# A four-layer graph network on one core: loading x ahead of more of the adjacency, transposing it later, and starting the second layer's rows before the first layer's last row tiles are evicted

## The reference

```
h = relu(layernorm(x))                      # layer 0
A = (adj != 0)
x = x + (A @ (h @ W + b)) / A.sum(axis=0)[:, None]
h = relu(layernorm(x))                      # layer 1
adj_hat = adj + I
d = adj_hat.sum(axis=1) ** -0.5
x = x + relu((adj_hat * d[:, None] * d[None, :]) @ (h @ weight))
```

## Time and profile before

| what | value |
|---|---|
| device time, median of 3 runs | 1339.97 us (1336.94 to 1341.37) |
| span of the profiled execution (first to last instruction) | 1337.7 us |
| PE busy | 1271.0 us, 95% |
| DVE busy | 1010.9 us, 76% |
| ACT busy | 629.3 us, 47% |
| POOL busy | 365.4 us, 27% |
| mean granted TensorE clock | 0.990 |

### The profile page before, as it was taken

The page is one execution under the profiler, slowest core; times in us unless marked ns, Lnnn a source line. Parts: engine busy times, 40 slices in busy tenths (PEclk is TensorE's granted clock), DMA queues, the critical chain, the costliest instruction groups (busy, mean ns, idle before and its releaser), DMA issues.

```text
span 1337.7 us, 26725 instructions
## 1 busy us (share of the span) xinstructions
PE 1271.0 (95%) x9548; PEld 947.8 (71%) x9548; DVE 1010.9 (76%) x2273; ACT 629.3 (47%) x1480; POOL 365.4 (27%) x422
## 2 busy tenths in 40 slices
PE   4899999998999999989999999999999987899998
PEld 3688888873455555557776777776767665688887
DVE  6899999939455555579988978978889987776642
ACT  3486644715322222266556755756666653311111
POOL 1100000013322222223323323332323222465433
PEclk8899999999999999999999999999999999999999
DMA  9999999702112210125653553543545414350500
GB/s 235 255 333 330 401 402 394 305 25 78 36 61 64 63 56 25 48 71 166 195 172 119 170 174 111 176 149 135 182 118 167 135 57 111 87 150 25 150 25 25
DMA packets 122898, 199.93 MB, mean 149 GB/s; under 512 B 13200, under 2 KB 83856, under 8 KB 122768
## 3 DMA queue, kind: packets, MB, share of 16 engines
q1 hardware_dynamic: 115568, 194.04, 45.6%
q10 hardware_dynamic: 7200, 4.20, 1.1%
HBM read 147.85 MB, written 50.33 MB: 148 GB/s over the span
## 4 chain that ended last, share of the span: by engine, by line
PE 69%; issue 13%; DVE 7%; POOL 6%; DMA 2%; ACT 1%; SPq 1%; ACTq 0%; POOLq 0%; DVEq 0%
PE ps L1817 10%; PE ps L1613 8%; PE ps L1614 8%; PE ps L1575 8%; PE ps L1576 8%; PE ps L1726 7%; PE ps L1711 5%; PE ps L1712 5%; POOL ring L687 4%; PE ps L1778 3%; PE ps L1743 2%; DMA acc<-in_adj 2%; DVE ring L789 1%; PE ps L1592 1%; POOL small L680 1%
## 5 line engine op out<-in xcount | busy, mean ns | idle before, releaser
L687 POOL TENSOR_TENSOR ring<-ring 128x512 f16<-128x512 f32 (+3 forms) x133 | 152.1, 1150 | 326.5 <-ACT ring L1487 326.5
L1575 PE MATMUL ps<-val_hi,ring 128*128 128x257 f16 x1024 | 227.1, 274 | 0.0
L1576 PE MATMUL ps<-val_lo,ring 128*128 128x256 f16 x1024 | 226.8, 273 | 0.0
L1613 PE MATMUL ps<-ring,acc 128*128 128x512 fp8e4 x512 | 194.1, 379 | 5.4 <-DVE acc L926 5.3
L1726 PE MATMUL ps<-hnt 128*128 128x512 f16 (+3 forms) x864 | 196.5, 364 | 1.0 <-DVE ring L1035 1.0
L1614 PE MATMUL ps<-ring,acc 128*128 128x512 fp8e4 x512 | 194.0, 379 | 0.0
L789 DVE STREAM_TRANSPOSE ring<-acc 128x1024 uint8<-128x1024 uint8 x128 | 151.4, 1219 | 20.4 <-DMA acc<-in_adj 20.2
L1711 PE MATMUL ps<-val_hi,ring 128*128 128x257 f16 x490 | 136.1, 278 | 18.9 <-POOL ring L687 12.9
L1711 PE MATMUL ps<-val_hi,hs 128*128 128x257 f16 x534 | 145.8, 273 | 0.9 <-DVE acc L1098 0.6
L1743 PE MATMUL ps<-val_hi,hs 128*128 128x257 f16 x534 | 145.8, 273 | 0.0
L1712 PE MATMUL ps<-val_lo,hs 128*128 128x256 f16 x534 | 145.6, 273 | 0.0
(11 more groups left out here) (234 smaller groups left out, 2377.3 us busy)
## 6 DMA issues: line engine op xcount, KB each, us to landing
acc<-in_adj SPq DMA_DIRECT2D x256, 256.0 KB, 7.5
turned_dram<-ring SPq DMA_DIRECT2D x56, 512.0 KB, 2.9
ring<-turned_dram SPq DMA_DIRECT2D x224, 128.0 KB, 2.9
at_dram<-ring SPq DMA_DIRECT2D x32, 512.0 KB, 8.9
ring<-at_dram SPq DMA_DIRECT2D x64, 256.0 KB, 4.0
ring<-at_dram SPq DMA_DIRECT2D x24, 512.0 KB, 3.9
ring<-at_dram SPq DMA_DIRECT2D x9, 1024.0 KB, 9.6
xs<-in_x SPq DMA_DIRECT2D x12, 256.0 KB, 12.3
```

The costliest lines, as they stand in the source:

```text
L687: nc.gpsimd.tensor_tensor(lo2[m % 2][:, k:GW], p2t[m % 2][:, k:GW], hi2[m % 2][:, k:GW], ALU.subtract).then_inc(sem["lo2_done"], 1)
L1575: nc.tensor.matmul(ps[:, k % 8, 0:D + 1], lhs, val_hi0[:, t, 0:D + 1], start=(t == 0), stop=False)
L1576: last = nc.tensor.matmul(ps[:, k % 8, 0:D], lhs, val_lo0[:, t, :], start=False, stop=(t == NB - 1))
L1613: nc.tensor.matmul(ps[:, bank + c, :], g_hi[:, t, c * P:(c + 1) * P], src, start=(t == 0), stop=False)
```

## The change

Both ends of layer 0 are edited.

First stage: SP's queue becomes x0, weights, x1, half 0, **x2**, half 1, **x3**, half 2, half 3, half 4 and so on. The quarters stand at the steps of a table `QUARTER_STEPS`: 9, 11, 15, 16, then one a step from 18 to 33, and two each in 34 and 35 (24 quarters, tiles 0 to 5). Tiles 6 and 7 and the two DVE column sums of group 0 follow the loop. An early tile is opened two steps after its last quarter (steps 18, 23, 27, 31 in place of 9, 13, 17, 21). ACT's 24 column sums of group 0 all stand behind the loop; before, they began at step 21.

Between the layers: DVE evicts only tiles 26 and 27 ahead of the degrees and the rows; tiles 28, 29, 30 and 31 are evicted after `low1` of batches 1, 3, 4 and 5. Before, 26 to 30 stood ahead of the rows, and 31 after batch 1. On POOL, `inverse_root` of the last group moves from before batch 3 to before batch 8, and the two `add_identity` from before batch 5 to behind the last batch.

```diff
--- before.py
+++ after.py
@@ -205,9 +205,16 @@
         ASUMS = NB - 4 * DSUMS
 
 
-        def quarters_by(s):
-
-            return s // 2 if s < 8 else s - 4
+        QUARTER_STEPS = (9, 11, 15, 16) + tuple(range(18, STEPS0)) + (STEPS0 - 2, STEPS0 - 1)
+        EARLY_TILES = len(QUARTER_STEPS) // 4
+
+        def quarters_in(s):
+
+            return [n for n, step in enumerate(sorted(QUARTER_STEPS)) if step == s]
+
+        def tile_step(b):
+
+            return sorted(QUARTER_STEPS)[4 * b + 3]
 
         def early_blocks():
 
@@ -216,7 +223,7 @@
             while total < GB * NB:
                 s, mine = len(table), []
                 for _ in range(5 if s < STEPS0 else GB * NB):
-                    open_b = [b for b in range(GB) if s >= 4 * b + 9 and progress[b] < min(NB, s - 4)]
+                    open_b = [b for b in range(GB) if s >= tile_step(b) + 2 and progress[b] < min(NB, s - 4)]
                     if open_b:
                         b = min(open_b, key=lambda b: (progress[b], b))
                         mine.append((b, progress[b]))
@@ -453,11 +460,11 @@
                 sp.dma_start(xs[32 * a:32 * a + 32, GB:8, :], x_q[a, :, GB:8, :]).then_inc(x_loaded[0], 16)
             load_x(sp, 1, (0, 2, 1, 3))
             load_half(sp, 0, (0, 2, 1, 3))
+            load_x(sp, 2, (0, 2, 1, 3))
             load_half(sp, 1, (0, 2, 1, 3))
-            load_x(sp, 2, (0, 2, 1, 3))
+            load_x(sp, 3, (0, 2, 1, 3))
             load_half(sp, 2, (0, 2, 1, 3))
             load_half(sp, 3, (0, 2, 1, 3))
-            load_x(sp, 3, (0, 2, 1, 3))
             for h in range(4, NH):
                 sp.wait_ge(sem["tr_done"], 2 * (h - 4) + 2)
                 load_half(sp, h, (0, 2, 1, 3))
@@ -638,14 +645,13 @@
                     inverse_root(g)
             inverse_root(NG - 2)
             for i, (t, n) in enumerate(batches1):
-                if i == 3:
+                if i == 8:
                     inverse_root(NG - 1)
-                if i == 5:
-                    add_identity(0)
-                    add_identity(1)
                 pool.wait_ge(sem["var1_ready"], i + 1)
                 nc.gpsimd.tensor_tensor(rstd4[i % 2][:, 0:n], ve4[i % 2][:, 0:n], half[:, 0:n],
                                         ALU.pow).then_inc(sem["rstd1_ready"], 1)
+            add_identity(0)
+            add_identity(1)
             pool.wait_ge(sem["r3_clamped"], 1)
             nc.gpsimd.tensor_tensor(f3, f3, half, ALU.pow).then_inc(sem["r3_ready"], 1)
 
@@ -816,15 +822,16 @@
             for s in range(STEPS0):
                 if s + AHEAD0 < NB:
                     stats0(s + AHEAD0)
-                for n in range(quarters_by(s), quarters_by(s + 1)):
+                for n in quarters_in(s):
                     transposed(n // 4, n % 4)
                 if s % GB == 2 and s // GB + 1 < NG:
                     shift0(s // GB + 1)
                 if 3 <= s < NB + 3:
                     low0(s - 3)
-                if s in (24, 30):
-                    column_sums(0, (s - 24) // 6, GW)
-
+            for k in range(EARLY_TILES, 8):
+                for i in range(4):
+                    transposed(k, i)
+                column_sums(0, k - EARLY_TILES, GW)
 
             dve.wait_ge(sem["w12_loaded"], 32)
             for l in (1, 2):
@@ -870,7 +877,7 @@
                     column_sums(k // GB - 1, k % GB, GW)
             dve.wait_ge(sem["tr_done"], 4 * NB)
             nc.vector.tensor_reduce(last_sum, at_bits[3][:, :, 3 * P:GW], AX.X, ALU.add).then_inc(sem["deg_step"], 1)
-            for k in range(NB - 6, NB - 1):
+            for k in range(NB - 6, NB - 4):
                 saved0(k)
 
 
@@ -925,14 +932,15 @@
                     dve.wait_ge(sem["hi1_ready"], t + 1)
                     nc.vector.tensor_tensor(g_lo[:, t, :], h1[t % 4], g_hi[:, t, :], ALU.subtract).then_inc(sem["g_ready"], 1)
 
+            saved_after = {1: NB - 4, 3: NB - 3, 4: NB - 2, 5: NB - 1}
             stats1(0)
             scales1(0)
             for i in range(len(batches1)):
                 if i + 1 < len(batches1):
                     stats1(i + 1)
                 low1(i)
-                if i == 1:
-                    saved0(NB - 1)
+                if i in saved_after:
+                    saved0(saved_after[i])
                 if i + 1 < len(batches1):
                     scales1(i + 1)
 
@@ -1383,9 +1391,7 @@
                         act.wait_ge(sem["wsc_ready"], 1)
                     nc.scalar.activation(val_hi0[:, t, 0:D], ps[:, 6 + t % 2, 0:D], ACT.Copy,
                                          scale=wsc).then_inc(sem["hi0_done"], 1)
-                if s >= 21:
-                    column_sum(0, 8 + s - 21, GW)
-            for t in range(24, NB):
+            for t in range(4 * DSUMS, NB):
                 column_sum(0, t, GW)
 
             for h in range(16, NH):
```

## The result

The changed kernel took 1318.19, 1320.16, 1320.20, 1339.48 and 1347.34 us: a median of 1320.20 against 1339.97 (both are medians of five executions, not of three as the section on the metric has it). The comparison leaves out executions more than 1.5% above the fastest, so its ratio of 0.984 (95% interval 0.982 to 0.987, about 1318.8 us) rests on the three lower ones. The same kernel timed a second time (run e1) took 1320.43 to 1342.21 us, six executions with a median of 1332.91 against 1341.2, ratio 0.991 (0.987 to 0.994). Over both times the eleven executions have a median of 1328.2, and five of them lie above 1337. The kernel before stayed between 1332 and 1351 beside every run, but for two outliers (1495.98 and 5717.65), with medians of 1338.8 to 1341.2. So the change is a gain of some 20 us in some executions and of nothing in others. Why it is both is the question of this study.

What follows compares the result with a forecast made beforehand. PE, busy 95% of the span, was taken as the bound. Gains of 10.4 us in layer 0's first stage and 5.3 between the layers, 15.7 in all, took 1339.97 to 1324.3 us; range 1319 to 1333.

Steps and rivals of the forecast that it cites:

- M(2): PE's projection early in layer 0's steps: forecast to start at 16.0 us in place of 22.68.
- The four half-clock steps: Layer 0's steps on PE: four assumed at half clock, 2.27 us each in place of 1.25, putting projection 17 at 43.5.
- lower bound of 41.4: Earliest start forecast for projection 17 on PE, 41.4 us, with only two half-clock steps right after the restart.
- the clock stays full: Rival for layer 0's steps: full clock after the restart, projection 17 at 41.4, total 1322.2 us; chance 0.17.
- M(17) to M(31), and the postponed pairs: Later steps of layer 0: 30.5 us between these projections; 36 more pairs follow afterwards, giving back 7.9 us.
- The cover: Layer 0 after the steps: DVE has adjacency tiles ready at least 10 us before PE wants them.
- The lead of the rows: Between the layers: DVE releases row tile 4 at 287.2, PE wants it at 292.5, a 5.3 us lead.
- DVE is late for the rows: Rival between the layers: lateness of DVE's last quarter beyond the 5.3 us lead is lost; chance 0.1.
- D of 10: Example lateness in us of DVE's last quarter of layer 0, giving a total of 1329.0 to 1330.3.
- The second part: Between the layers: later evictions and identity remove PE's waits for `low1`, a gain of 5.3 us.
- The slower rival: Layer 0's load stream: its low rate lasts longer, last quarter over 21 us late, the change loses; chance 0.04.

Runs made afterwards that it cites:

- e8: Changed kernel plus eight unread 512 KB DRAM-to-DRAM copies on SP's queue, one behind each of halves 24 to 31: median 1339.18 us.
- e4: Changed kernel with the old load order, x2 back behind half 1 and x3 behind half 3: median 1332.40 us.
- e11: Changed kernel with the later layers' weights loaded early and the cast adjacency's stores spread behind every second half: median 1324.49 us.
- e10: Changed kernel with each group's four stores of cast adjacency spread behind every second half: median 1330.41 us.
- e13: Changed kernel with every group's stores of cast adjacency issued eight halves later: median 1331.72 us.
- e14: Changed kernel with every group's stores eight halves later and the later layers' weights loaded early: median 1323.30 us.
- e3: Kernel before with only the edit between the layers (later evictions, inverse root and identity), old steps and loads: median 1334.58 us.
- e2: Changed kernel with the edit between the layers undone, leaving only the first-stage edit: median 1327.36 us.

## Why the prediction was wrong

The forecast was 1324.3 in a range of 1319 to 1333. The ratio of the undisturbed executions gives 1318.8, just below the range; the median of all eleven, 1328.2, is inside. Two errors of opposite sign stand behind this: a clock penalty of 4.1 us that did not come, which made the undisturbed executions faster than forecast, and a cover of at least 10 us that was not there, which made the others slower. That the median of all lies within 4 us of the forecast is luck.

**M(2), confirmed.** At 16.53, forecast 16.0.

**The four half-clock steps, refuted.** This is the step of the prediction that failed: a term of the sum, priced at 4.1 us (four steps of 2.27 us in place of 1.25), that measured nothing. From M(2) to M(17) after took 22.56 us where the same working without half clock gave 23.35. M(17) was at 39.09, not 43.5, and below even the lower bound of 41.4, which had two such steps for a restart. The granted clock is 1.00 from 12.5 on. The rival "the clock stays full" was right, and more so than it was written, since it still had two such steps; e8, with about one and a half, is nearest to it. The mistake was to take the fall at 35.11 over into a stretch that has no such waits. That fall stood behind two waits before consecutive projections, 1.45 us before the one at 32.84 and 0.95 before 35.11; in e4 it was 1.92 and 0.72 us before 29.72. In after no wait in the steps is above 0.94 us. A single wait of 1.78 us left the clock full in e11, and one of 2.26 us did not in e8. What the clock goes by, one wait or several together, these few falls do not settle. The wait of e11:

```profile
16.01 1.10 PE L1598 MATMUL ps<-w_all,hs 128*128 128x256 f32 x4 [1.78 <-DVE val_lo L799]
```

The Trainium skill (TensorE: Matmul & The Clock Gate, "Why this matters for your kernels") asks for one idle gap longer than any of these; e11 agrees with it, the falls of before, of e4 and of e8 do not.

**M(17) to M(31), and the postponed pairs, confirmed.** 30.19 us, forecast 30.5. So M(31) came 4.7 us before the 74.0. Tile 4 began at 84.39 in after, 15.1 us behind M(31), where it was 7.2 us in before (99.56): the 7.9 us given back for the postponed pairs are right. In e11 it was at 68.69 and PE left layer 0 at 280.0, 211.3 us later; the forecast had 285.6 - 74.0 = 211.6. So the 28 tiles of 7.0 us are right as well, where no quarter is late.

**The cover, refuted in part.** "So it reaches tile 8 about when it did" came true (100.60 in after, forecast 99.57). What failed is "tile 31 at 279, ready at 263.1": tile 16 was already 12.0 us late (166.68 against 154.68). It took the load stream of one execution for a fixed thing, and that is the least repeatable part of the kernel: the last quarters stood anywhere from 257.5 to 280.9 among the runs on one queue without added traffic and without another order of quadrants. The kernel before had some 21 us of slack there (268.08 against 289.12), so all its executions looked alike, and nothing in one trace of it told of the spread. The "at least 10 us of cover" fell to nothing in after, e1, e10 and e13, with 4.4 to 7.1 us of waits for quarters.

**The lead of the rows, confirmed in its mechanism, mis-sized by the first error.** Tile 4 was to be released 26.5 us behind the last quarters (287.2 - 260.7). In e14, with the last quarters at 260.71 as before, DVE released it here, and PE took it there:

```profile
287.37 1.42 DVE L934 TENSOR_TENSOR acc<-hs,acc 128x256 f16<-128x256 f32 x4
```

```profile
287.84 0.39 PE L1620 MATMUL ps<-ring,acc 128*128 128x512 fp8e4 x1 [1.26 <-DVE acc L934]
```

The release is right to 0.2 us. The lead of 5.3 us was reckoned from PE's end at 285.6; with full clock PE was done at 279.3 and waited 1.26 us. What the clock gave ate the lead that was to cover a late stream. That is why each us past some 260 counts in full from there on: the rival "DVE is late for the rows" is what happened in the profiled executions of after and e1, and by their times in five of the eleven. Its rule, that all beyond the lead is lost, holds; its chance of 0.1 was too small, and its D of 10 is 18 in after and 20 in e1. It put the cause in stage buffers freed later, and no run shows that.

**The second part, confirmed:** 5.9 us in e3 and in e11, forecast 5.3.

**The slower rival** named the first store to DRAM as what might start the high rate; e13 and e14 show the step moving with it. But the change did not move that step: it comes at 72 us in before and at 75 in after.

**The sum, without the two errors:** 1324.3 - 4.7 for the clock gives 1319.6 for a stream as early as that of before, and e14 is at 1319.5. For a stream D later, less the 0.6 us of lead that is left (5.3 - 4.7), it gives 1337.1 for after (D = 18.1) and 1339.2 for e1 (20.2). They are at 1339.5 and 1342.1, 2.4 and 2.9 us above, and both have matmuls of 634 ns behind the waits, where the clock is down.

What stays open is why the stretches behind 105 us differ from execution to execution: 377 GB/s in before and 318 in after from 99.8 to 200, at the same share of busy engines and with the same queue. It wasn't settled either whether the change itself makes them likelier: e2, with the same steps, had 371 and e1 339 GB/s from 72 to 255. The fast and the slow stretches are there in both kernels; the change is what makes them count.
